# A two-layer graph network: the convolution moved from count steps 8 to 17 to steps 5 to 13, an eighth first sum among the last eleven count steps, degrees summed in four column groups, ScalarE's table loaded at its head

## The reference

```python
h = relu(layernorm(x))
# layer 0
xn   = batchnorm(h, norm1)                      # over the 1250 nodes
agg  = segment_sum(xn[src], dst) / maximum(deg, 1)[:, None]
conv = relu(agg @ W_conv + b_conv)
# attention of 8 heads on the first 256 nodes (random features, 256 per head), then @ Wo
x = x + batchnorm(conv + h_attn + h, norm2)
# layer 1
h = relu(layernorm(x))
agg = segment_sum(h[src], dst)
h = relu(batchnorm(((1 + eps) * h + agg) @ W1 + b1))
x = x + relu(batchnorm(h @ W2 + b2))
```

## Time and profile before

| | before |
|---|---|
| median of 3 runs | 365.79 us (365.54 to 367.07) |
| profiled execution | 365.55 us, span 363.7 us |
| granted TensorE clock | 0.998 |
| TensorE busy | 348.0 us, 96% of the span |
| VectorE busy | 246.4 us, 68% |
| ScalarE busy | 181.3 us, 50% |
| GpSimd busy | 95.2 us, 26% |

### The profile page before, as it was taken

How to read it: one execution, slowest core, us unless ns; L and a number is a source line. 1 busy time by engine, 2 the same in 40 slices (tenths; PEclk the granted TensorE clock), 3 DMA queues, 4 the chain that set the end, 5 groups by cost and what they waited for, 6 DMA issues and landing times.

```text
span 363.7 us, 6194 instructions
## 1 busy us (share of the span) xinstructions
PE 348.0 (96%) x2072; PEld 224.0 (62%) x2072; DVE 246.4 (68%) x667; ACT 181.3 (50%) x302; POOL 95.2 (26%) x163
## 2 busy tenths in 40 slices
PE   7899899989999999999998999999999999999994
PEld 3678655757777666767564675455555555565562
DVE  5889999998998995867998787522464443422325
ACT  0548538768477167454437766411534645233132
POOL 8132120000000000100042778722277465101100
PEclk9999999999999999999999999999999999999999
DMA  6990303300000000034900000000000000010223
GB/s 162 289 303 30 119 1 119 118 3 1 3 3 4 3 3 3 3 97 148 264 9 3 0 2 3 2 2 1 2 0 0 2 0 2 0 51 21 70 58 85
DMA packets 13539, 18.05 MB, mean 50 GB/s; under 512 B 1839, under 2 KB 6895, under 8 KB 13491
## 3 DMA queue, kind: packets, MB, share of 16 engines
q1 hardware_dynamic: 12538, 17.21, 16.4%
q10 hardware_dynamic: 953, 0.23, 0.3%
HBM read 14.88 MB, written 2.56 MB: 48 GB/s over the span
## 4 chain that ended last, share of the span: by engine, by line
PE 74%; DVE 15%; issue 4%; ACT 3%; DVEq 2%; DMA 0%; POOL 0%; SPq 0%; ACTq 0%; POOLq 0%
PE bank L1424 71%; DVE ring L988 2%; DVE st L1095 2%; DVE st_row L938 2%; PE bank L1815 1%; PE bank L1454 1%; PE bank L1774 1%; ACT hn L688 1%; DVEq L1137 1%; DVE st_row L1310 1%; DVE x L1305 1%; DVE mv_row L939 1%; DVE x L1375 0%; PE bank L1635 0%; DVE ln_tmp L933 0%
## 5 line engine op out<-in xcount | busy, mean ns | idle before, releaser
L1424 PE MATMUL bank<-AT,hh 125*128 125x400 f16 (+3 forms) x250 | 81.2, 332 | 1.2 <-DVEq L1335 0.4
L1424 PE MATMUL bank<-AT,hl 125*128 125x400 f16 (+3 forms) x250 | 80.9, 332 | 0.0
L988 DVE TENSOR_SCALAR ring<-iota_code,code 125x250 f16<-125x250 f16 x200 | 46.1, 307 | 1.4 <-issue 1.4
L1424 PEld LDWEIGHTS bank<-AT,hh 125*128 125x128 f16 x250 | 24.1, 97 | 19.8 <-issue 1.1
L1424 PEld LDWEIGHTS bank<-AT,hl 125*128 125x128 f16 x250 | 24.2, 97 | 17.6 <-issue 0.2
L1424 PE MATMUL bank<-ring,S 125*128 125x250 f16 x200 | 33.5, 310 | 0.0
L1424 PE MATMUL bank<-a_hi,w_hi 128*128 128x400 f16 (+1 forms) x96 | 32.6, 340 | 0.0
L1424 PE MATMUL bank<-agg_hi,w_hi 128*128 128x400 f16 (+1 forms) x96 | 32.6, 339 | 0.0
L1424 PE MATMUL bank<-agg_hi,w_lo 128*128 128x400 f16 (+1 forms) x96 | 32.5, 339 | 0.0
L1424 PE MATMUL bank<-a_hi,w_lo 128*128 128x400 f16 (+1 forms) x96 | 32.5, 339 | 0.0
L1424 PE MATMUL bank<-agg_lo,w_hi 128*128 128x400 f16 (+1 forms) x96 | 32.5, 339 | 0.0
(11 more groups left out here) (229 smaller groups left out, 703.0 us busy)
## 6 DMA issues: line engine op xcount, KB each, us to landing
w_s<-w SPq DMA_DIRECT2D x4, 1024.0 KB, 5.2
x_in<-x SPq DMA_DIRECT2D x5, 448.0 KB
x<-x SPq DMA_DIRECT2D x2, 1120.0 KB
out<-x SPq DMA_DIRECT2D x6, 224.0 KB
wB<-wk SPq DMA_DIRECT2D x1, 1024.0 KB, 9.6
wA<-wq SPq DMA_DIRECT2D x1, 1024.0 KB, 13.8
wC<-w_conv SPq DMA_DIRECT2D x1, 1024.0 KB, 16.1
wB<-wv SPq DMA_DIRECT2D x1, 1024.0 KB, 6.3
```

Source lines behind the costliest of these rows:

```text
L988: return dve.tensor_scalar(ring[:, slot, j, a:b], iota_code[0:CH, a:b], code[:, bass.ds(c + j, 1)], float(-CODES * t), ALU.subtract, ALU.i ...
L1424: return pe.matmul(o, l, r, start=start, stop=stop, skip_group_check=True)
```

## The change

1. `SLOTS` is written anew. In short (slot numbers from 0): `hT5 hT6 N1` go from slot 2 to slot 1, everything up to `UK0` is done by slot 2; `V0 V1` at slots 3 and 4; `MX0 G0` at slot 5, `QT0 UK1 G1` at slot 6, then one `G` per slot, two in slot 10, `G9` in slot 13 (before: `G0` in slot 8, `G9` in slot 17). The first sums stand in slots 14 to 25, eight of them (`A31` is new there; before seven, in slots 19 to 25).
2. A degree is summed by 40 matmuls of a quarter of the columns each, four at a time into four groups of 32 partitions (`D`), VectorE takes the reciprocal of 113 or 100 columns instead of 450 or 400 (`rdq`), and a new piece `E` spreads it to all partitions with 4 float32 matmuls, which ScalarE copies to `rdb`.
3. ScalarE loads its table of functions ahead of everything, and issues its four small DMAs once the edges have landed.
4. `SPARE["ranges"]`, matmuls that only keep TensorE busy, 3 instead of 5; `normed(i+2)` on ScalarE and `normed_parts(i+2)` on VectorE stand just ahead of taking `Gi` out.

```diff
-    "hT0 hT1 hT2 K0 RG K1", "hT3 hT4 PT Q0", "hT5 hT6 N1 Q1", "hT7 hT8 N0 hT9 UK0", "FR P", "UQ0 V0", "MX0 V1", "QT0",
-    "G0 UK1", "KV0 UQ1 G1", ...
+    "hT0 hT1 hT2 K0 RG K1", "hT3 hT4 PT Q0 hT5 hT6 N1", "Q1 hT7 hT8 N0 hT9 UK0", "FR P V0", "UQ0 V1", "MX0 G0",
+    "QT0 UK1 G1", "KV0 G2", ...
+    "KV3 F1", "A21", "O3", "TA0 TA1 A31 WO0 WO1")]
+SQ_AT, SPLIT_AT, H_AT = 2, 4, 4
+SPARE = {"start": 20, "ranges": 3, "hT0": 3, "hT1": 3, "hT2": 4}
+LONE_FROM = 6
-LAST = "A31 F2 D2 A02 A12 A22 A32 A33".split()
+LAST = "D2 F2 A02 E2 A12 A22 A32 A33".split()
+def quarters(c):
+    c0, w = COLS[c]
+    q = -(-w // 4)
+    return [min(g * q, w - q) for g in range(4)], q
...
-            act.wait_ge(sem("s_const"), NCONST)
+            act.wait_ge(sem("s_ones"), 1)
+            act.activation(tables[:], ones16[:, 0:1], ACT.Relu).then_inc(sem("s_tables"), 1)
+            act.wait_ge(sem("d_edge"), 64)
...
+                if name[0] == "E":
+                    act.activation(rdb[:, c0:c0 + w], ps[:, 0:w], ACT.Copy).then_inc(sem("s_rdb"), 1)
+                    act.wait_ge(sem("s_rdb"), c + 1)
+                    act.sem_inc(free[PLACE[name][0]], 1)
...
             weight_mean(1)
+            counts_out("E2")
             for half in range(2):
                 weight_high(1, half)
...
+                    ps = read_group(dve, name)[:, 0:quarters(c)[1]]
+                    if c:
+                        dve.wait_ge(full[PLACE[f"E{c - 1}"][0]], PLACE[f"E{c - 1}"][1] + 1)
                     own.step(dve.tensor_scalar(d, ps, 1.0, wscale[:, 0:1], ALU.max, ALU.mult))
+                    dve.reciprocal(d, d).then_inc(sem("s_rdq"), 1)
...
-                own.after(n_deg[0])
+                dve.wait_ge(sem("s_rdb"), ci + 1 if ci < NC else NC)
...
+                    starts, w = quarters(int(name[1]))
+                    places = [ps[g * 32:(g + 1) * 32, 0:w] for g in range(4)]
+                    blocks = [slice(c0 + s, c0 + s + w) for s in starts]
+                    ins = sum_up([[(o, ones16[0:L, 0:32], AT[:, k, b]) for o, b in zip(places, blocks)] for k in range(T)],
+                                 [(o, ones16[0:L, 0:32], ATlo[:, k, b]) for k in range(T) for o, b in zip(places, blocks)])
+                elif name[0] == "E":
+                    c = int(name[1])
+                    starts, w = quarters(c)
+                    pe.wait_ge(sem("s_rdq"), c + 1)
+                    ps = open_group(pe, name)
+                    for g, s in enumerate(starts):
+                        ins = mm(ps[:, s:s + w], ident[:, 32 * g:32 * g + 1].broadcast_to([P, P]), rdq[:, 0:w], True, True)
```

More of the change, by code:

```diff
@@ L76 @@
 SLOTS = [s.split() for s in (
[4 rows of a table removed]
-SQ_AT, SPLIT_AT, H_AT = 2, 6, 6
-SPARE = {"start": 20, "ranges": 5, "hT0": 3, "hT1": 3, "hT2": 4}
-LONE_FROM = 8
[4 rows of a table added]
+SQ_AT, SPLIT_AT, H_AT = 2, 4, 4
+SPARE = {"start": 20, "ranges": 3, "hT0": 3, "hT1": 3, "hT2": 4}
+LONE_FROM = 6
 COUNT_BANK = [t % 2 if t < LONE_FROM else 0 for t in range(NW)]
@@ L322, in gnn_kernel @@
         rdb = place("rdb", [P, N], F32, 146)
+        rdq = place("rdq", [P, -(-COLS[0][1] // 4)], F32, 152)
         x1 = place("x1", [L, T, D], F32, 154)
@@ L753, in _ @@
             for t in range(len(SLOTS)):
-                if t == H_AT:
-                    normed(0)
                 for name in [n for n in SLOTS[t] if not late(n)] if t else ():
@@ L764, in _ @@
                     elif name[0] == "G":
+                        if int(name[1]) + 2 < T:
+                            normed(int(name[1]) + 2)
                         conv_high(int(name[1]))
-                    elif name[0] in "AD":
+                    elif name[0] in "AE":
                         counts_out(name)
+                    elif name[0] == "D":
+                        pass
                     else:
@@ L774, in _ @@
                     conv_weights()
-                if t == H_AT + 1:
+                if t == H_AT:
+                    normed(0)
                     normed(1)
@@ L788, in _ @@
                 for name in SLOTS[t]:
-                    if name[0] == "G" and int(name[1]) + 2 < T:
-                        normed(int(name[1]) + 2)
-                for name in SLOTS[t]:
                     if late(name):
@@ L1033, in attention @@
                 elif name[0] == "D":
-                    c0, w = COLS[int(name[1])]
+                    c = int(name[1])
+                    d = rdq[:, 0:quarters(c)[1]]
                     dve.wait_ge(sem("s_bn1"), 1)
-                    d = rdb[:, c0:c0 + w]
-                    if name in LAST:
-                        ps = read_group(dve, name)[:, 0:w]
-                    else:
-                        dve.wait_ge(free[PLACE[name][0]], PLACE[name][1] + 1)
-                        ps = d
+                    ps = read_group(dve, name)[:, 0:quarters(c)[1]]
+                    if c:
+                        dve.wait_ge(full[PLACE[f"E{c - 1}"][0]], PLACE[f"E{c - 1}"][1] + 1)
                     own.step(dve.tensor_scalar(d, ps, 1.0, wscale[:, 0:1], ALU.max, ALU.mult))
-                    n_deg[0] = own.mark(dve.reciprocal(d, d))
-                    if name in LAST:
-                        dve.sem_inc(free[PLACE[name][0]], 1)
+                    dve.reciprocal(d, d).then_inc(sem("s_rdq"), 1)
+                    dve.sem_inc(free[PLACE[name][0]], 1)
+                elif name[0] == "E":
+                    pass
                 elif name[:2] == "WO":
@@ L1209, in piece @@
                 elif name[0] == "G":
+                    if int(name[1]) + 2 < T:
+                        normed_parts(int(name[1]) + 2)
                     conv_low(int(name[1]))
@@ L1257, in _ @@
                        .then_inc(sem("s_wcl"), 1)
-                if 0 < t - H_AT - 1 < T:
-                    normed_parts(t - H_AT - 1)
+                if t == H_AT + 1:
+                    normed_parts(1)
                 for name in SLOTS[t]:
@@ L1576, in attention @@
                     ps = open_group(pe, name)
-                    ins = accumulate([(ps[:, 0:w], [(ones16[0:L, :], AT[:, k, c0:c0 + w]) for k in range(T)],
-                                       [(ones16[0:L, :], ATlo[:, k, c0:c0 + w]) for k in range(T)])])[0]
+                    starts, w = quarters(int(name[1]))
[3 more added lines that the diff above has]
+                                 [(o, ones16[0:L, 0:32], ATlo[:, k, b]) for k in range(T) for o, b in zip(places, blocks)])
+                elif name[0] == "E":
+                    c = int(name[1])
+                    starts, w = quarters(c)
[3 more added lines that the diff above has]
+                        ins = mm(ps[:, s:s + w], ident[:, 32 * g:32 * g + 1].broadcast_to([P, P]), rdq[:, 0:w], True, True)
                 elif name[0] == "N":
@@ L1682, in accumulate, with sum_up @@
                 return last
+            def sum_up(steps, extra):
+                for o, l, r in steps[0]:
+                    mm(o, l, r, True, False)
+                with pe.If_lt(big_r, most_r):
+                    for o, l, r in extra:
+                        mm(o, l, r, False, False)
+                pe.end_ifs()
+                for n, step in enumerate(steps[1:]):
+                    for o, l, r in step:
+                        ins = mm(o, l, r, False, n == len(steps) - 2)
+                return ins
             seen = pe.alloc_register("seen")
```

8 lines of the change are left out of this document (3 added, 5 removed), and 11 rows, old and new, of tables (LONE_BANKS, SLOTS).

## The result

The changed kernel takes **376.6 us** (median of 6 runs, 373.9 to 377.4) against 365.9 for the kernel before in the same comparison: 1.028 times as long, 95% interval 1.026 to 1.031, that is +10.7 us. The forecast was 369.1 (366.4 to 371.6). The direction was right, the size was not. The profiled execution took 377.43 us with a span of 375.6.

A forecast was written before the change was run, and what follows sets the result against it. The prediction took TensorE's work up to the end of layer 0's sums as the bound. Its terms, 0.7 - 1.1 + 0.4 - 0.1 + 3.5 = +3.4 us on 365.55, gave 369.0, put down as 369.1 (366.4 to 371.6).

The forecast's parts named there:

- What bounds the kernel: Up to the end of layer 0's sums: TensorE works nearly without a gap, and its total ends them.
- Term 1: Slot 1: `hT5` waits for the copy of `hT3` with the count step still to do, +0.7 us.
- Term 2: Slots 2 to 5: old waits of 1.5 and 0.46 go, new ones at `FR` and `G0` come, -1.1 us.
- Term 3: Slot 6: `UK1` waits 2.4 us for ScalarE's exponentials, later waits of 1.6 and 0.4 go, +0.4 us.
- Term 4: Degrees up to slot 19: cheaper `D` plus `E` against full sums, with a 0.7 wait at `E0`, -0.1 us.
- Term 5: Tail of layer 0: `E2` waits about 3.8 us for VectorE's reciprocal behind the statistics, +3.5 us in all.
- Behind layer 0 nothing is changed: Everything after layer 0: no change in time, so no term for it in the sum.
- The table load at nothing: Start of the kernel: earlier first transposes and `K0` only make `hT5` wait longer, priced at nothing.
- The four early DMAs at nothing: ScalarE's early DMAs: small, no cost in the sum; any delay of VectorE's row statistics left to the range's upper end.
- ScalarE was not in time for `UK1`: Slot 6, a rival: ScalarE's exponentials are over in time for `UK1`, without the 2.4 us wait, 366.6 us; 11%.
- the column groups ran side by side: Degrees, a rival: column groups run one behind another, each `D` 1.9 instead of 0.5 us, 371.8 us; 8%.
- there was no further wait in the dense slots: Slots 5 to 13, a rival: VectorE or ScalarE late for several `G` by a few tenths, 370 to 372 us; 6%.

The follow-up runs named there:

- e11: e12 with `hT5 hT6 N1` put back from slot 1 to the head of slot 2: 365.6 us, 0.999 of the kernel before.
- e12: e6 with a never-taken branch over 27 matmuls ahead of `E2`, which moves TensorE's later instructions: 366.4 us.
- e15: The kernel before with only ScalarE's table load moved to its head: 365.7 us, ratio 1.000.
- e5: The changed kernel with 54 idle register moves on TensorE, of which the compiled program holds one, so the changed kernel once more: 376.4 us.
- e7: The changed kernel with VectorE's maximum and reciprocal of `D2` right behind `WO1`, ahead of the eight statistics: 370.6 us.
- e9: The changed kernel with a never-taken branch over 27 matmuls ahead of `E2`, so that TensorE's later instructions lie 56 places later: 374.2 us.
- e4: The changed kernel with ScalarE's four small DMAs issued behind the constants again, as before the change: 376.9 us.
- e13: The changed kernel with `UK1` a slot later, `hT5` back in slot 2, and the degrees as before (full sums and full reciprocals): 368.6 us.
- e6: The changed kernel with `UK1` one slot later and `D2`'s maximum and reciprocal ahead of VectorE's eight statistics: 370.7 us.

## Why the prediction was wrong, step by step

- **What bounds the kernel**: right. TensorE nearly without a gap up to the end of layer 0's sums; each wait put there came through to the end.
- **Term 1** (+0.7): right in the medians. e11 against e12 measures 0.8. The wait itself was 1.7 to 2.0 us, since TensorE also came to it sooner (e15 shows that part), and in 2 of 11 profiles (e5, e7) the clock fell behind it.
- **Term 2** (-1.1): 0.5 to 0.9 too hopeful; `G0` came at 55.15 in the profiled execution and at 54.73 in e9, forecast 54.2. The 0.4 between the two are the late row statistics (20.48 for 20.07, see e4). The new waits ahead of `FR` and `G0` are there (0.18 and 0.65 for 0.5 and 0.4), and one of 0.36 ahead of `N0` that was not forecast.
- **Term 3** (+0.4): the wait was sized to a hundredth (2.38 for 2.4), and failed in its **price**: behind it came 1.65 us of lower clock, in all seven profiles that have this wait.
- **Term 4** (-0.1): the sizes of the parts are right (0.56 for 0.5 for the sum `D2`, 0.87 to 0.98 for 0.9 an `E`, the wait at `E0` 0.49 for 0.7). Three misses. One is that between matmuls on the full array a `D` costs more than its own time. The changed kernel's rows, and then e13's:

```profile
132.17 0.35 PE L1438 MATMUL bank<-AT,hl 125*128 125x450 f16 x1
132.45 0.62 PE L1438 MATMUL bank<-AT,ones 125*32 125x100 f16 x40
133.23 1.36 PE L1438 MATMUL bank<-ring,S 125*128 125x250 f16 x8 [0.15 <-issue]
```

```profile
127.76 0.35 PE L1438 MATMUL bank<-AT,hl 125*128 125x450 f16 x1
127.95 1.85 PE L1438 MATMUL bank<-AT,ones 125*128 125x400 f16 x10
129.64 0.58 PE L1438 MATMUL bank<-ring,S 125*128 125x250 f16 x3
```

`D1` starts 0.09 late and is followed by the count step after 0.78 instead of 0.56, where the full-width sum has no gap; `D0` shows 0.09 and 0.15. That is 0.31 and 0.24 us, close to the estimate of 0.3 per `D` that the prediction left out of its sum. With it the degrees up to slot 19 came to +0.5 and not -0.1. The second miss is that `D1` now shares bank 6 with `O2`, which waits 0.42 us for it. The third: the sentence that the 6 us saved on VectorE buy nothing was true of the stretch it named but not of the tail: with the full reciprocal of `D2` VectorE, and then `x0`, is late (e13, 3.0 us with the clock).
- **Term 5** (+3.5): the wait was 3.38 for 3.8, and from the end of `WO1` to `x0` all went as forecast but for the clock: 1.7 us more. `x0` follows `E2`'s start by 16.74 us in the changed kernel (185.53 to 202.27) and by 15.06 in e9, where the clock did not fall.
- **"Behind layer 0 nothing is changed"**: this failed. Nothing is changed in the source, but TensorE's instructions lie elsewhere, and the wait behind the jump in the last tile cost 1.8 us, of which 0.4 replace a wait that the kernel before has a little later (0.43 at 229.10, for VectorE), and 1.7 of lower clock behind it. This was the step of which the profile of before had no row.
- The table load at nothing: right (e15). The four early DMAs at nothing: no gain from taking them back is seen (e4), but a few tenths stay open. The rivals: ScalarE was not in time for `UK1`, the column groups ran side by side, and there was no further wait in the dense slots.

The sum for the profiled execution, 377.43 - 365.55 = 11.9: forecast 3.4, three falls of the clock 1.65 + 1.7 + 1.7, the wait in layer 1 net 1.35, `G0` late by 0.95, the degrees 0.6, `O2` 0.4; that is 11.75, and 0.1 to 0.2 I can't place.

The steps that failed are therefore two. Terms 3 and 5 had the waits right and their price wrong: the prediction took a wait to cost its own length, without writing this down, and each of the two was followed by 1.65 to 1.7 us of lower clock. And the term for all behind layer 0, put at nothing, measured 3.1 us in the profiled execution.

By experiments the 11.0 us between the changed kernel and e11 are 5.9 for `UK1` and `E2` (e6), 4.3 for the instructions' place with the clock behind it (e12) and 0.8 for `hT5` (e11). These steps can't be split finer by medians, since the clock falls in some executions and not in others.

## What to carry to other kernels

Price a new wait of TensorE by its length and, where it is about 2 us or longer, by up to another 1.7 us for the clock behind it; a wait filled with matmuls that nobody reads costs only its length (3.3 us here for two waits). When a change adds or removes some hundred instructions ahead of a long untaken branch, look in the profile after for an idle stretch called issue between two matmuls that nothing separates, and move the code before you judge the change. And ask of a reciprocal or any small result that another engine waits for, what stands ahead of it in its own engine's order: one piece moved (e7) was worth 6 us in the medians, about 5 of them the wait and the clock behind it.
